# Adding the causal mask of the first attention in four 64 by 64 quadrants of TensorE's array

## The reference, cut to what matters

```
q = (x @ Wq).reshape(b, n, 16, 64).transpose(0, 2, 1, 3) * scale
kv = concat([null_kv, x @ Wkv], axis=1)
sim = einsum('bhid,bjd->bhij', q, kv)
sim = where(causal_mask, -finfo.max, sim)
attn = softmax(sim, axis=-1)
out = einsum('bhij,bjd->bhid', attn, kv)
return out.reshape(b, n, 16 * 64) @ Wout
```

## Time and profile before

| what | value |
| --- | --- |
| median of 3 runs | 1343.27 us (1342.66 to 1344.61) |
| the profiled execution's own time | 1342.8 us |
| its span | 1341.0 us |
| PE busy (matmul) | 1116.9 us, 83% |
| DVE, ACT, POOL busy | 58%, 49%, 25% |
| first attention, first to last instruction | about 10.8 to 130.8 us |
| TensorE clock, mean | 0.904 of full speed |

### The profile page before, as it was taken

How to read it: one execution, slowest core, us unless ns; L and a number is a source line. 1 busy time by engine, 2 the same in 40 slices (tenths; PEclk the granted TensorE clock), 3 DMA queues, 4 the chain that set the end, 5 groups by cost and what they waited for, 6 DMA issues and landing times. The chain is left out here.

```text
span 1341.0 us, 25706 instructions
## 1 busy us (share of the span) xinstructions
PE 1116.9 (83%) x9898; PEld 721.7 (54%) x9899; DVE 775.2 (58%) x1948; ACT 660.2 (49%) x1386; POOL 332.5 (25%) x320
## 2 busy tenths in 40 slices
PE   6898784598889975779869865979889988798998
PEld 4565563346666642347527634847434444475776
DVE  4565546586665478867886786546362565453111
ACT  2564343463452245777686662535656443345332
POOL 1333200023210026464564520240000034700000
PEclk9999897599899977869978995889899989899999
DMA  7000000200000000000000000080196710000000
GB/s 304 1 2 2 1 3 0 97 0 1 3 1 1 1 1 0 1 2 1 1 1 2 1 0 1 2 339 14 31 193 127 159 17 1 2 3 1 1 0 16
DMA packets 18329, 44.83 MB, mean 33 GB/s; under 512 B 4992, under 2 KB 8096, under 8 KB 17568
## 3 DMA queue, kind: packets, MB, share of 16 engines
q1 hardware_dynamic: 18208, 43.20, 11.2%
HBM read 42.41 MB, written 0.79 MB: 32 GB/s over the span
## 5 line engine op out<-in xcount | busy, mean ns | idle before, releaser
L930 ACT ACTIVATE L_xattn_pT<-banks 128x512 f32<-128x512 f32 x128 | 69.0, 598 | 87.9 <-PE banks L808 87.9
L241 POOL TENSOR_TENSOR norm_rstd<-norm_var,norm_power 128x4 f32<-128x4 f32 x24 | 24.6, 1026 | 345.9 <-DVE norm_var L234 345.8
L991 DVE TENSOR_REDUCE L_xattn_top<-banks 128x4 f32<-128x512 f32 x128 | 79.5, 684 | 36.3 <-PE banks L776 36.3
L1576 DVE TENSOR_TENSOR L_ffn_a<-L_ffn_a,L_ffn_share 128x512 f32<-128x512 f32 x64 | 39.9, 685 | 61.0 <-DMA L_ffn_share<-L_ffn_shares 60.6
L1803 ACT ACTIVATE L_ffn_aT<-banks,L_ffn_shift 128x512 f32<-128x512 f32 x64 | 43.3, 687 | 58.9 <-PE banks L1755 57.3
L1490 PE MATMUL banks<-L_ffn_a,region_a 128*128 128x512 f32 x136 | 67.5, 601 | 5.1 <-DVE L_ffn_a L1576 5.1
L1816 DVE SCALAR_TENSOR_TENSOR x<-banks,L_ffn_combine,x 128x128 f32<-128x128 f32 x64 | 18.0, 344 | 88.7 <-PE banks L1766 88.7
L1481 PE MATMUL banks<-hT,region_a 128*128 128x512 f32 x136 | 68.8, 611 | 0.0
L1766 PEld LDWEIGHTS banks<-region_b,L_ffn_aT 128*128 128x128 f32 x512 | 59.4, 192 | 6.7 <-issue 6.7
L490 ACT ACTIVATE L_attn_p<-banks,L_attn_shift 128x129 f32<-128x129 f32 x128 | 45.4, 369 | 33.0 <-DVE L_attn_shift L540 33.0
L1755 PE MATMUL banks<-hT,region_b 128*128 128x512 f32 x128 | 59.6, 609 | 0.0
(11 more groups left out here) (546 smaller groups left out, 2890.8 us busy)
## 6 DMA issues: line engine op xcount, KB each, us to landing
L_ffn_share<-L_ffn_shares SPq DMA_DIRECT2D x32, 512.0 KB, 10.8
region_b<-in_L_ffn SPq DMA_DIRECT2D x1, 6216.0 KB, 30.1
region_a<-in_L_ffn SPq DMA_DIRECT2D x1, 4416.0 KB, 13.2
region_b<-in_L_attn SPq DMA_DIRECT2D x1, 3150.5 KB, 10.5
region_a<-in_L_ffn SPq DMA_DIRECT2D x1, 3080.5 KB, 21.2
region_b<-in_L_attn SPq DMA_DIRECT2D x1, 1633.5 KB, 9.1
region_b<-in_L_xattn SPq DMA_DIRECT2D x1, 835.0 KB, 9.7
w_tables<-in_tables SPq DMA_DIRECT2D x1, 832.0 KB, 12.6
```

Of the source, the lines that this page charges most:

```text
L930: nc.scalar.activation(pT[:, n % 2, 4 * i:4 * i + 4, :], rows_of(flip[i][:], 4), ACT.Exp, scale=scale).then_inc(exped, 1)
L991: nc.vector.tensor_reduce(top[:, 32 * i:32 * i + 32:HD], rows_of(score[i][:], 4), X, ALU.max).then_inc(topped, 1)
L1576: nc.vector.tensor_tensor(a[:, k % AHEAD, :], a[:, k % AHEAD, :], share[:, batch % RING, j, :], ALU.mult).then_inc(weighed, 1)
```

## The change

The mask of each bank is added in two products instead of one, each in a 64 by 64 quarter of the array. Quarter (a, c) takes its data from partitions 64a to 64a + 63 and writes to partitions 64c to 64c + 63 of bank k + a. Where a equals c the rows come from `causal`; where it does not, the mask rows that are wanted lie in the other half of the partitions, so there is a second copy, `crossed`, whose halves are exchanged. Two more transfers of 64 rows by 512 bytes bring the exchanged halves from the packed constants into a free piece of `region_a` (`g.halves`), and POOL casts them to bf16 with one memset and one cast ahead of its wait for the weights.

```diff
 sp.dma_start(g.x[:], g.dram["x"].rearrange("b t d -> t b d")).then_inc(g.x_loaded, 16)
+at = g.const.places["neg_causal"][0]
+for a in range(2):
+    sp.dma_start(g.halves[64 * a:64 * a + 64, :],
+                 g.dram["const"][64 - 64 * a:128 - 64 * a, at:at + T]).then_inc(g.halves_loaded, 16)
 sp.dma_start(ctx[:], g.dram["ctx_1024"].rearrange("b t d -> t b d")).then_inc(loaded, 16)
...
 nc.gpsimd.memset(causal[:, T:W], 0.0)
 nc.gpsimd.tensor_copy(causal[:, 0:T], g.causal_bf[:, 0, :]).then_inc(null_ready, 1)
+pool.wait_ge(g.halves_loaded, 32)
+nc.gpsimd.memset(crossed[:, T:W], 0.0)
+nc.gpsimd.tensor_copy(crossed[:, 0:T], g.halves).then_inc(null_ready, 1)
 pool.wait_ge(w.loaded, 16)
...
-for a in range(2):
-    nc.tensor.matmul(bank[k + a][:, 0:2 * W], g.ident_bf[:], bc(causal[:], 1, 2), start=True, stop=False,
-                     skip_group_check=True)
+for c in range(2):
+    for a in range(2):
+        rows = slice(64 * a, 64 * a + 64)
+        mask = causal if a == c else crossed
+        nc.tensor.matmul(bank[k + a][64 * c:64 * c + 64, 0:2 * W], g.ident_bf[rows, rows], bc(mask[rows, :], 1, 2),
+                         start=True, stop=False, skip_group_check=True)
...
-pe.wait_ge(null_ready, 2)
+pe.wait_ge(null_ready, 3)
...
+g.halves, g.halves_loaded = g.region_a[:, 8192:8320], nc.alloc_semaphore("halves_loaded")
```

More of the change, by code:

```diff
@@ L286, in multi_query_attention @@
     qT, kvT, kv = st.sb("qT", [128, NH // 2, TOK]), st.sb("kvT", [128, B, W]), st.sb("kv", [T, B, DH])
-    causal, null_wide = st.sb("causal", [T, W], BF16), st.sb("null_wide", [128, T])
+    causal, crossed, null_wide = st.sb("causal", [T, W], BF16), st.sb("crossed", [T, W], BF16), st.sb("null_wide", [128, T])
     top, shift, sums, inv = (st.sb(s, [T, 4, Q]) for s in ("top", "shift", "sums", "inv"))
```

## The result

The changed kernel takes 1353.04 us (median of 17 runs, 1349.34 to 1359.99), the kernel before 1347.87 (17 runs, the three shown above among them, 1340.93 to 1354.40): ratio 1.0044, interval 1.0026 to 1.0061. It is slower by 5.2 us, where 1344.8 was forecast, 1.5 above the median shown, and the range ended at 1348.4. The kernel before came out 4.6 us above its earlier median in this series, so the ratio is what counts: 1.0044 against the forecast's 1344.8 / 1343.27 = 1.0011. The profiled execution of the changed kernel took 1350.4.

What follows compares the result with a forecast made beforehand. PE was taken as all but the limit, with both masks on the first attention's period loop. Profiled 1342.8 plus 1.2 (masks) and 0.35 (start) gave 1344.35; the median's 0.47 made it 1344.8 us, range 1342.0 to 1348.4.

Steps and rivals of the forecast that it cites:

- masks on the loop of the period: First attention: both masks of a 5.50 us period lie on the loop setting its length; mask time moves it equally.
- Entering, 0.20: PE, last pass to first mask product: changing shape from 128*128 to 64*64 takes 0.20 us in place of 0.12.
- The four quarters together, 0.11 and 0.02: Mask on PE: all four quarter products run together, one 260-column stream of 0.11 us plus 0.02 stagger.
- the rival in which the second pair waits: Mask on PE: second two quarters follow the first, +0.15 us a unit, 1348.4 us in all; chance 15%.
- Leaving, 0.09: PE, mask to scores: changing shape from 64*64 to 64*128 loses 0.09 us.
- the rival without this gap: PE, mask to scores: no gap from 64*64 to 64*128, 0.16 us less a unit, 1339.3 us; chance 8%.
- The load in the open, 0.05: Mask on PE: the new shape's first weights can't be loaded ahead, which exposes 0.05 us a unit.
- the lower end, 0.01: Low estimate of the mask's exposed weight load, 0.01 us, from bf16 products in 32-row tiles.
- The start, 0.35: Ahead of the attention: added transfers, memset and cast delay the whole stage by 0.35 us, between 0.2 and 1.0.
- the local sum, 1.55: Whole kernel: the forecast's added time, 1.2 us for the masks and 0.35 us for the start.
- All later blocks start later and stay as they are.: Blocks behind the first attention: they begin later but keep their lengths, so add no time of their own.

Runs made afterwards that it cites:

- the 64-row version: Changed kernel with each bank's mask in two products of 64 rows by 128 columns, exchanged copies loaded and cast later; 1347.22 against 1348.67, ratio 0.9995.
- the padding alone: Kernel before with 32 tiny products (128 instructions) added on PE ahead of the first work on the context; 1351.76 against 1348.23, ratio 1.0028.
- the split at the delta rule: Kernel before with 32 tiny products added at the head of the delta rule's stage; 1348.57 against 1349.23, ratio 0.9994.

## Why the prediction was wrong

**What bounds the kernel** was read rightly: masks on the loop of the period. Taking 0.11 out of the scores and the gap out of the mask in the 64-row version brought the attention from 120.77 to 118.56.

**Entering, 0.20**: right (0.21). **The four quarters together, 0.11 and 0.02**: right; they begin within 0.01, and the rival in which the second pair waits fell (it wanted a period of 5.8). The Trainium skill's rule behind that rival ("TensorE: Matmul & The Clock Gate", Part 3, loads overlap only when the row group differs) doesn't make quarters over the same rows follow one another here. **Leaving, 0.09**: right; the rival without this gap fell (it wanted a period below 5.4). What it promised is seen in another pair: from 64*128 to 64*128, with another type, there is no gap and the load is hidden, and the stage was 2.2 us shorter, where 2.6 was expected of that mask.

**The load in the open, 0.05**, was mis-sized: 0.02. The float32 row it was taken from was dearer than what bf16 shows here; the lower end, 0.01, came from a bf16 row and was the nearer one. A unit is 0.44, not 0.47, and the period 5.53, not 5.58. The attention's stage grew by 0.50, where 1.2 for the masks and 0.15 for POOL's part of the start were in the sum.

**The start, 0.35**: right in size, in part by luck. The context came 0.20 late as forecast (L180, the old L176, begins at 7.76 against 7.56), and L447 begins 0.41 late. But POOL's longer list was to be the last thing waited for, with L346's counterpart at 11.77; POOL was ready at 11.62, the cast taking its lower figure, 0.29, and the weights, thought to be 0.20 late, held it until 11.82. Alone, the start costs nothing that 12 runs can tell (0.9997).

So the local sum, 1.55, was really 0.7 in the profile. The step that failed is the last one ahead of the sum: **"All later blocks start later and stay as they are."** They don't. 64 products more in PE's list move every later instruction by 128 places, and with that the lengths of blocks that nobody touched: +6.9 between the two profiled executions, 3.5 by the runs of the padding alone, 5.7 by taking it out of the changed kernel again, against 0.7 for the mask and the start. The forecast missed the measured difference, 5.2, by 3.6. None of the rivals had it, though the page of before had the queue that brings the instructions and its 79 packets.

How far is that shown? That the place in the list moves these blocks, and not the mask, its result or the later start: by padding that computes nothing and does to before what the change does, by the same padding that undoes it in the changed kernel, and by the split at the delta rule. That it goes by pieces of 256 instructions, 16 KB: by the return at exactly 256, tried with two masks, by no return at 64, 128 or 192, and by the stops at one place within 256, in eleven of 14 traces. The number of pieces isn't it: 79 packets at no shift, 80 at 16 KB, with one set of lengths. That the time follows: for 8 KB by four ratios whose intervals lie above one (1.0044, 1.0027, 1.0023, 1.0028), but not for the 64-row mask (0.9995), not for 4 and 12 KB, whose intervals hold one, and not for the padding at the delta rule. And the way is open: a shift moves PE's stops, but in the marked blocks these cost time where there is no shift; the two that grew did so by the clock, and why the clock is lower where PE has waited the same 1.32 ahead of it, no run here tells. Neither was it tried whether two masks of 64 rows can go into one bank without the exchanged copy.

## What to carry to other kernels

A change that adds or removes instructions on an engine with a long straight list is two changes: its own, and the shift of everything behind it. Here the second was the larger one, 3.5 to 5.7 us against 0.7, and it can hide a mask whose own stage is 2 us shorter. Before such a change is thrown away or kept, bring what stands behind it to the same place of the list, up to whole pieces of 256 instructions, with tiny work in an idle stretch at the head, and compare again; blocks of unchanged code whose lengths changed are the sign to look for. And count changes of array shape on the engine that bounds: here a product in the shape of its neighbour cost its stream alone, 0.11, and each change of shape about 0.09 more.

## What the runs showed of the hardware

- The same code, shifted by 4, 8 or 12 KB in TensorE's list, takes 90.7 to 90.8, 63.8 to 64.0 and 138.8 to 139.9 us in three blocks (92.5 once for the first), and 89.2, 65.0 to 65.6 and 136.9 to 137.7 unshifted or shifted by 16 KB.
- TensorE stopped for 0.04 to 0.66 us with nothing shown to wait for, in eleven of 14 traces, always at one place within each 256 instructions of its list; one packet of 16 KB came for each 256.
- A block of 137 us whose code is unchanged took 137, 139 or 142 us with 13.7, 17.1 or 20.5 us of it at 1.2 GHz.
- A stage of full-array products began at a mean granted clock of 0.59 over 3.42 us in one place and 1.00 in the other, behind the same wait of 1.32.
- Four 64 by 64 products in the four quarters of the array begin within 0.01 and last up to 296 ns each for 260 bf16 columns, where the full product lasts 273.
- Between products of the same tile shape there is no gap when bf16 is followed by float32: 0.11 for 260 columns at 2.4 GHz.
